# A two-layer decoder on one core: the experts' gate and up weights as stationary operand, head foldings in column halves, one bias product, halved row sums

## What is computed

```python
# layer 0: mixing over time, then attention on a context, then experts
out = jnp.einsum('bes,st->bet', x, Wr + Wc) + bias
...
for e in range(n_experts):                       # 8 experts, one per token
    m = (expert_idx == e)[:, None]
    xe = jnp.where(m, xs, 0.0)
    h = jax.nn.silu(xe @ gate_w[e]) * (xe @ up_w[e])
    out = out + jnp.where(m, h @ down_w[e], 0.0)
# layer 1: Fourier attention, latent attention, ternary feed-forward
q_big = jnp.einsum('bshk,hkq->bshq', q_hk, w_kc_q)
q_r = jnp.einsum('bshq,hqr->bhsr', q_big, W_qr)
k_r = jnp.einsum('bld,hdr->bhlr', kv_rope, W_kr)
scores = jnp.einsum('bhsr,bhlr->bhsl', q_r, k_r)
...
inv = jax.lax.rsqrt(jnp.mean(hf * hf, axis=-1, keepdims=True) + eps)   # rms_norm of h
```

## Time and profile before

| | |
|---|---|
| median of 3 runs | 703.32 us (700.88 to 707.11) |
| profiled execution | 706.16 us |
| its span in the profile | 704.9 us |
| PE busy | 595.1 us, 84% |
| mean granted TensorE clock | 0.935 of 2.4 GHz |

### The profile page before, as it was taken

One profiled execution on the slowest core, in us unless ns is written; L12 is line 12 of the kernel. 1 busy time (PEld: TensorE's weight loads), 2 busy tenths in 40 slices (PEclk: granted clock), 3 DMA queues, 4 the chain that ended last, 5 costly groups with the idle time before them and its releaser, 6 DMA issues.

```text
span 704.9 us, 14612 instructions
## 1 busy us (share of the span) xinstructions
PE 595.1 (84%) x5393; PEld 460.6 (65%) x5393; DVE 503.4 (71%) x1297; ACT 408.1 (58%) x914; POOL 357.3 (51%) x405
## 2 busy tenths in 40 slices
PE   4888788998898775899267789999989999999996
PEld 3655566776666553555233578888768777978885
DVE  3766557776787787556279867777888879968475
ACT  2765456665677752444173356666675766578374
POOL 2435665765549870000398933264484543245565
PEclk9998899999999898999767799999999999999999
DMA  7642212423023422231501000001101010000001
GB/s 235 191 150 75 71 43 85 113 81 99 24 76 124 135 96 90 90 99 61 153 27 45 16 1 2 1 1 32 31 1 31 1 31 3 1 1 2 1 1 61
DMA packets 50416, 41.98 MB, mean 60 GB/s; under 512 B 15513, under 2 KB 48794, under 8 KB 50330
## 3 DMA queue, kind: packets, MB, share of 16 engines
q1 hardware_dynamic: 48810, 36.85, 17.7%
q0 software_dynamic: 1536, 4.20, 1.8%
HBM read 31.72 MB, written 10.35 MB: 60 GB/s over the span
## 4 chain that ended last, share of the span: by engine, by line
PE 42%; DVE 7%; ACT 5%; issue 4%; POOL 2%; DMA 0%; POOLq 0%; DVEq 0%; ACTq 0%
PE bank L1032 8%; PE bank L1034 7%; PE bank L1033 7%; PE bank L1450 6%; PE bank L1039 4%; PE bank L1214 3%; DVE wide L1763 1%; ACT wide L1589 1%; PE bank L1432 1%; PE bank L1315 1%; PE bank L1290 1%; PE bank L1317 1%; PE bank L1288 1%; PE bank L1287 1%; PE bank L1286 1%
## 5 line engine op out<-in xcount | busy, mean ns | idle before, releaser
L1763 DVE TENSOR_TENSOR first<-bank,first 128x512 f16<-128x512 f32 (+3 forms) x113 | 65.3, 592 | 19.4 <-ACT first L1656 6.3
L1039 PE MATMUL bank<-c_identity,wide 128*128 128x128 f32 (+2 forms) x267 | 46.4, 295 | 34.3 <-ACT wide L1589 17.8
L2220 POOL TENSOR_TENSOR first<-first 128x512 f16<-128x512 f32 x44 | 53.0, 1208 | 37.6 <-ACT first L1650 32.4
L1039 PEld LDWEIGHTS bank<-c_identity,wide 128*128 128x128 f32 (+2 forms) x267 | 32.7, 149 | 42.7 <-ACT wide L1589 19.2
L1763 DVE TENSOR_TENSOR wide<-bank,wide 128x512 f16<-128x512 f32 (+3 forms) x85 | 47.0, 566 | 16.1 <-ACT wide L1629 8.5
L1039 PE MATMUL bank<-c_identity,first 128*128 128x128 f32 (+2 forms) x297 | 48.2, 285 | 7.7 <-DVE first L1949 2.4
L2244 POOL DMA_INDIRECT wide<-made_rows,made_at x8 | 8.1, 1007 | 75.3 <-DMA made_rows<-wide 73.5
L1039 PEld LDWEIGHTS bank<-c_identity,first 128*128 128x128 f32 (+2 forms) x297 | 33.7, 140 | 15.3 <-DVE first L1949 3.0
L2200 POOL TENSOR_TENSOR first<-first,minus_half 128x2 f32<-128x2 f32 x30 | 21.5, 717 | 27.8 <-DVE first L1872 27.8
L1032 PE MATMUL bank<-wide,first 128*128 128x256 f16 (+3 forms) x115 | 28.1, 260 | 7.2 <-DVE first L1763 5.9
L2319 POOL TENSOR_TENSOR wide<-wide 128x512 f16<-128x512 f32 x16 | 18.0, 1124 | 31.2 <-ACT wide L1739 31.2
(11 more groups left out here) (509 smaller groups left out, 2249.0 us busy)
## 6 DMA issues: line engine op xcount, KB each, us to landing
wide<-in_L_xattn_Wq SPq DMA_DIRECT2D x9, 256.0 KB, 3.1
wide<-in_L_ffn_gate_w SPq DMA_DIRECT2D x8, 256.0 KB
wide<-in_L_ffn_up_w SPq DMA_DIRECT2D x8, 256.0 KB
wide<-in_L_ffn_down_w SPq DMA_DIRECT2D x8, 256.0 KB
wide<-in_L_xattn_Wo SPq DMA_DIRECT2D x16, 128.0 KB
wide<-in_L_ffn_w_gate_up SPq DMA_DIRECT2D x8, 256.0 KB
first<-in_x SPq DMA_DIRECT2D x7, 256.0 KB, 5.0
x_mid<-first SPq DMA_DIRECT2D x7, 256.0 KB, 3.2
```

Source lines behind the costliest of these rows:

```text
L1039: last = nc.tensor.transpose(view[0:m, c0:c0 + n], src, kc["identity" if dt == F32 else "identity_bf"][0:n, 0:n])
L1763: return V.tensor_tensor(lo, whole, hi, ALU.subtract)
L2220: G.tensor_tensor(B.pl[r], B.pf, B.ph[r], ALU.subtract).then_inc(says("ex_l"), 1)
```

## The change

- Experts: `x_gu` takes the weights as stationary operand, in m = 0 to 3 (two slices of 128 columns of gate, two of up) and c = 0, 1, and the turned tokens as moving one. Its output has h's columns on the partitions, as `x_dn` needs it; `x_b` goes, and `x_b_hi`, `x_b_lo` read h from SBUF.
- Foldings: `hk` turns both heads at once; `hb` puts the two heads on partitions 0 to 63 and 64 to 127 of one bank; `hc` multiplies both by a block-diagonal `krT` (128x128), whose two blocks `hk_c` writes in two copies into zeros set once.
- Bias: it is held on 128 partitions, the high half in row 0, the low in row 1, zeros below, and one matmul adds both.
- `rm`: `ss` of g = 3 also adds the two halves of its 512 columns, and `rm` has half as many matmuls.
- The planner's lengths for these parts are changed, and with them the order of all parts.

```diff
-    p.add("pm_b", 0, 0, "POOL", 110, [("pm_pow", 0, 0)], -10)
+    p.add("pm_b", 0, 0, "POOL", 230, [("pm_pow", 0, 0)], -10)
...
-            p.add("hb", 0, i, "PE", 186, [("ha_c", 0, i)], rank, 1, ("hb_c", 0, i))
+            p.add("hb", 0, i, "PE", 110, [("ha_c", 0, i)], rank, 1, ("hb_c", 0, i))
...
-        chain("x_b", n, 0, [("x_h", n, 0)], k, pe=32, hi=38, lo=42)
+        p.add("x_b_hi", n, 0, "ACT", 38, [("x_h", n, 0)], k)
+        p.add("x_b_lo", n, 0, "DVE", 40, [("x_b_hi", n, 0)], k)
...
-        flip(bank("hk", 0, j), [(n * DC, R, W.kr[:, n, :]) for n in range(HEADS)]).then_inc(says("hk"), 1)
+        flip(bank("hk", 0, j), [(0, P, W.kr.rearrange("p h n -> p (h n)"))]).then_inc(says("hk"), 1)
...
-        for n in range(HEADS):
-            for q in range(2):
-                last = mm(b[0:R, n * D:(n + 1) * D], W.qr[:, q, n, :], k.t1[:, n, q, :], start=(q == 0), stop=(q == 1))
+        for q in range(2):
+            for n in range(HEADS):
+                last = mm(b[n * R:(n + 1) * R, 0:D], W.qr[:, q, n, :], k.t1[:, n, q, :], start=(q == 0), stop=(q == 1))
...
-            for n in range(HEADS):
-                mm(b[:, (2 * c + n) * DC:(2 * c + n + 1) * DC], k.t2[:, n * D + c * P:n * D + (c + 1) * P], k.krT[:, n * DC:(n + 1) * DC],
-                   start=True, stop=True)
+            mm(b[:, c * P:(c + 1) * P], k.t2[:, c * P:(c + 1) * P], k.krT, start=True, stop=True)
...
-                    for half in range(2):
-                        last = mm(o, kc["all_ones"][0:1, :], k.bias[half], start=False, stop=(half == 1))
+                    last = mm(o, kc["all_ones"], k.bias, start=False, stop=True)
...
-        for c in range(C):
-            last = mm3(b[:, :], cut(X.xT, ALL, slice(c * P, (c + 1) * P)), tuple(w[:, c * 2 * D:(c + 1) * 2 * D] for w in gu), c == 0, c == C - 1)
+        for m in range(2 * C):
+            for c in range(C):
+                at = c * 2 * D + m * P
+                last = mm3(b[:, m * P:(m + 1) * P], tuple(w[:, at:at + P] for w in gu), cut(X.xT, ALL, slice(c * P, (c + 1) * P)), c == 0, c == C - 1)
...
-            for n in range(2):
-                last = mm(b[:, t:t + 1], B.ss[:, n * S + t * P:n * S + (t + 1) * P], k.one, start=(n == 0), stop=(n == 1))
+            last = mm(b[:, t:t + 1], B.ss[:, t * P:(t + 1) * P], k.one, start=True, stop=True)
...
     def hk_c(u, j):
         act.wait_ge(*done("hk", 0, j))
-        fn(k.krT, bank("hk", 0, j)[0:R, 0:HEADS * DC], ACT.Copy).then_inc(says("hk_c"), 1)
+        act.wait_ge(*done("pm_pow", 0))
+        for n in range(HEADS):
+            own = slice(n * R, (n + 1) * R)
+            last = fn(k.krT[own, n * DC:(n + 1) * DC], bank("hk", 0, j)[own, 0:DC], ACT.Copy)
...
-        fn(k.t2, bank("hb", 0, j)[0:R, :], ACT.Copy).then_inc(says("hb_c"), 1)
+        fn(k.t2, bank("hb", 0, j)[:, 0:D], ACT.Copy).then_inc(says("hb_c"), 1)
...
+        G.memset(k.krT, 0.0)
...
+        pool.step(G.memset(k.bias, 0.0))
+        pool.step(G.tensor_copy(rows, pre.bias))
+        pool.step(G.tensor_scalar(pre.rest, rows, kc["identity"][0:2, 1:2], None, ALU.mult))
+        G.tensor_tensor(rows, pre.bias, pre.rest, ALU.subtract).then_inc(says("pm_b"), 1)
...
+        last = G.tensor_tensor(B.ss, B.ss, B.s1, ALU.add)
+        if g == 3:
+            pool.step(last)
+            last = G.tensor_tensor(B.ss[:, 0:S], B.ss[:, 0:S], B.ss[:, S:2 * S], ALU.add)
+        last.then_inc(says("ss"), 1)
```

More of the change, by code:

```diff
@@ L141 @@
               "fold_dve": ("hq_lo", "ho_lo"), "ternary_dve": ("f_sc", "f_gt"), "route_dve": ("rt_top", "rt_hot", "rk_seen", "rk_slot"), "gate_act": ("rt_gate", "rt_xs"), "table_dve": ("tb_cnt", "tb_tile", "tb_tok"),
-              "expert_pe": ("x_t", "x_gu", "x_b", "x_dn"), "expert_act": ("x_t_hi", "x_tan", "x_b_hi", "x_out"),
+              "expert_pe": ("x_t", "x_gu", "x_dn"), "expert_act": ("x_t_hi", "x_tan", "x_b_hi", "x_out"),
               "expert_dve": ("x_t_lo", "x_h", "x_b_lo")}
@@ L325, in lay_plan @@
             before = [("ho_lo", 0, i - 1)] if i else []
-            p.add("hk", 0, i, "PE", 25, [("in_h", 0, i), ("in_mix", 0, 0)] + before, rank, 1, ("hk_c", 0, i))
-            p.add("hk_c", 0, i, "ACT", 30, [("hk", 0, i)], rank)
+            p.add("hk", 0, i, "PE", 16, [("in_h", 0, i), ("in_mix", 0, 0)] + before, rank, 1, ("hk_c", 0, i))
+            p.add("hk_c", 0, i, "ACT", 50, [("hk", 0, i), ("pm_pow", 0, 0)], rank)
             p.add("ha", 0, i, "PE", 190, [("in_h", 0, i), ("in_mix", 0, 0)] + before, rank, 2, ("ha_c", 0, i))
@@ L655, in program @@
     k.t1 = wide.tile([HEADS, 2, D], F32, 96)
-    k.t2 = wide.tile([2 * D], F32, R)
+    k.t2 = wide.tile([D])
     k.t3 = wide.tile([2 * D])
-    k.krT = sb("krT", [R, HEADS * DC])[:]
+    k.krT = sb("krT", [P, P])[:]
     wide_end = wide.at
@@ L668, in program @@
     pre.dv = wide.tile([2])
-    pre.bias = wide.tile([S], F32, 1)
+    pre.bias, pre.rest = wide.tile([S], F32, 2), wide.tile([S], F32, 2)
     pre.ones32 = wide.tile([P])
@@ L860, in ld_mix @@
         load(pre.wrow, A["L0_attn_weight"][1:2, :].broadcast_to([P, S]), dma["mix"])
[L861 removed]
+        load(pre.bias, A["L0_attn_bias"].rearrange("(a n) -> a n", a=1).broadcast_to([2, S]), dma["mix"])
         for c in range(C):
@@ L1464, in tensor_program @@
     parts = {f.__name__: f for f in (pm_mm, pt, pd, po, pb, hk, ha, hw, hb, hc, fw, turn, ctx, kv, proj, q, max, mt, sc, pv, ot, rt, rk, sh, tb,
-                                     x_t, x_gu, x_b, x_dn, ft, kt, cs, vt, gu, rm)}
+                                     x_t, x_gu, x_dn, ft, kt, cs, vt, gu, rm)}
     for name, u, g in k.plan.order["PE"]:
@@ L1692, in x_b_hi @@
     def x_b_hi(n, g):
-        act.wait_ge(*done("x_b", n))
-        fn(k.X[n % ELANES].hT[0], bank("x_b", n)[:, 0:D], ACT.Copy).then_inc(says("x_b_hi"), 1)
+        act.wait_ge(*done("x_h", n))
+        fn(k.X[n % ELANES].hT[0], k.X[n % ELANES].h, ACT.Copy).then_inc(says("x_b_hi"), 1)
     def x_out(n, g):
@@ L2095, in x_b_lo @@
         dve.wait_ge(*done("x_b_hi", n))
-        rest(X.hT[1], bank("x_b", n)[:, 0:D], X.hT[0]).then_inc(says("x_b_lo"), 1)
+        rest(X.hT[1], X.h, X.hT[0]).then_inc(says("x_b_lo"), 1)
     def kt_lo(u, g):
```

21 lines of the change are left out of this document (8 added, 13 removed).

## The result

The changed kernel takes 725.33 us (median of 4 runs, 724.08 to 728.65), the kernel before on the same chip 704.53 us. The ratio is 1.031, with a 95% interval of 1.027 to 1.035: slower by 21.6 us, 18.7 to 24.5 on 705. The forecast was 716, slower, with a range of 703 to 729. The profiled execution has a span of 725.1 us where that of before had 704.9.

The account below looks back on a forecast made before the run. PE was taken to lead, with its sequencer's issue bounding the changed experts. Experts +17, clock +1, foldings and bias -4.5, second layer -1 sum to +12.5 us; on 703.3 that gives 716, range 703 to 729.

Parts of the forecast that it names:

- +17 for issue: Expert stage: register instructions make PE's issue the bound, 3.33 us a tile, 84 us for 67.
- +1 for the clock: Expert stage: short falls of PE's granted clock add 1 us.
- issue is hidden: Rival, `x_gu`: a full queue hides issue and the array alone counts, total 694, band 688 to 696; chance 0.08.
- Half clock: Rival, expert stage: clock at 1.2 GHz in part or full, total 725 to 741; chance 0.09.
- Weight loads as the bound: Rival, `x_gu`: weight loads of 0.10 us each set the pace, total 718 at most; chance 0.04.
- The reordered second layer: Rival, second layer: its new order costs its upper bound, total 722; no chance of its own given.
- Foldings and bias: First stretch: PE does 12.7 us less, a third counted, -4.5 us, bounds 0 and -12.7.
- Second layer: Second layer: halved `rm`, longer `ss` and moved order together give -1 us.
- For seven units it lies beside `proj` 3: Second layer: the `ss` fold, 0.65 us on POOL, delays `rm` only in the last unit, +0.5 us with its wait.
- I count -2.5: Second layer: half the `rm` passes go, -3.9 us on PE in all, of which 2.5 counted.
- the order moves here as well, I put +1: Second layer: the moved order of the same parts costs +1 us, between -3 and +7.
- issue-bound experts: Expert stage: the main case, PE's issue sets the pace, total 710 to 725; chance 0.67.

Follow-up runs that it names:

- e6: Changed kernel with expert 0 as a constant for every tile on PE, so no number is loaded or checked and no register instructions remain in the experts: 700.41 us.
- e9: Kernel before with the work of the change's foldings and bias, all planner lengths as before, so the old order: 706.12 us, ratio 1.0004.
- e12: Changed kernel with the old work of foldings and bias, new planner lengths kept, so the changed kernel's order: 734.53 us, ratio 1.045.
- e10: Kernel before, same order, with one more 128x256 fold on POOL at the end of the last `ss`, its result unused: 709.09 us.
- e4: Changed kernel with its halved `rm` and fold in `ss`, but the planner's lengths for both as before: 721.18 us.
- e5: Kernel before with all work as it was, only the planner's lengths of `rm` and the last `ss` set to the new ones: 710.26 us.
- e1: Changed kernel with the experts' part undone, old `x_gu` and `x_b` back: 714.34 us, ratio 1.013.
- e8: Kernel before with foldings and bias of the change, nothing else, in an order of its own: 713.51 us, ratio 1.010.
- e11: Kernel before with foldings and bias of the change and another set of planner lengths, chosen so that the laid out plan is shorter: 714.50 us.
- e2: Kernel before with the experts' part of the change alone: 731.94 us, ratio 1.039.
- e7: Changed kernel with the 23 experts' numbers loaded by three instructions ahead of the first `x_gu`, still 23 checks: 722.34 us, ratio 1.023.

## Why the prediction was right, and where it was not

**The experts: right, by its own steps.** Forecast +17 for issue and +1 for the clock, measured +18.1. A register instruction costs 0.125 us of issue (threes 0.25 apart), the numbers are 368 for 92, and e6 takes the whole away without touching a matmul. A tile takes 3.31 us without waits, for my 3.33, and the waits for DVE and ACT are 3.6 us, for the 4 that I kept. Inside the tile two small errors cancelled: loading and checking takes 0.80 us for my 0.68, and the 0.15 for `x_t` and banks was not needed. The granted clock was 0.98 for 1.00 before: it stood at 0.50 up to 276 us, so the matmuls of the first `x_gu` start 0.107 us apart and it takes 2.5 us for 2.0 by issue. That is half of the +1; from 280 us on the clock was full.

**The rival "issue is hidden": fell** as its own condition said; 0.125 us is not below 0.078. What it would have given is e6: 700.4 measured (694 forecast), the stage 8.8 us shorter than before. The array's share of that is the 4 us of the rival's sum; most of the rest is waits and issue, about 7 us in the stage before and 2.5 in e6. **Half clock: fell** at 0.98 for the stage. **Weight loads as the bound: fell** at 56 ns a matmul in e6. **The reordered second layer, 722:** this one came nearest, with +6.4 us; but the order is only a part of it.

**Foldings and bias: the term of PE right, its share of the end not.** Forecast 12.7 us off PE, measured 13.5; `hb` 1.08 us for 1.15, the four passes of `hc` 0.71 for 0.63. "Of these I count a third" was a guess at how much reaches the end, and there is no such share: in the old order 0 (e9, within 2 us), in the new order some 10, 4 to 16 by the intervals (e12). The sum's -4.5 lies between, and the trace's -2.5 in the stage table is within what one trace can be off.

**Second layer: wrong, -1 forecast, +6.4 measured.** Its stretch was to be shorter by 0 to 5 us. Three steps of it failed, and one was missing. "For seven units it lies beside `proj` 3": the fold took 0.73 us for my 0.65, but PE's waits on `ss` grew from one of 0.6 us to several of 3.6 to 4.5 us, and the layer by 2.1 (e10). I had looked at where the fold stands beside PE's work in the last unit, and not at how little room there was between `ss` and `rm` in the others. "I count -2.5" for the halved `rm`: e4 is not shorter than e10 (350.8 and 350.2), so in the order of before nothing of it is left. The missing step answers for most of it: I took the clock of the last unit for full, and its fall costs e4 1.7 us and e10 nothing, so without it e4 would be about 1 us the shorter one. And "the order moves here as well, I put +1": 2.9 to 3.7 us (e5, after to e4), inside the -3 to +7 that I had given, but that end deserved more weight: of the five new orders in the study (after, e1, e5, e8, e11) none had a shorter second layer.

**Stores and gather, "which the change leaves alone"**: 1.8 us shorter, 15.3 for 17.1. It is 15.2 to 15.8 us in all kernels of the study but before, e2, e5 and e10 (16.6 to 17.3). Those four have the old foldings and bias, but so has e12 with 15.5, and e9 with the old order has 15.3; I can't say why.

The sum of the misses is the difference: 12.5 forecast, and 0.1 more in the experts, 2.0 in the first stretch, 1.8 less behind the experts and 7.4 more in the second layer make 20.2, the difference of the two spans but for rounding.

**The total** was inside the range, 9 us above the 716. It lies at the upper edge of the 710 to 725 that I gave to issue-bound experts, and by the letter in the band of the half clock, 725 to 741, which did not happen. The sum with the second layer at its upper bound gave 722; above that the range rested on the slower clock, so part of the hit is luck: the experts' mechanism and size were right, the second layer's sign was not.

## What to carry to other kernels

Where an operand's address comes from a register, count the distinct slices and not the matmuls: turning the weights into the stationary operand cut them into 16 slices a tile where 4 were enough, and at 0.125 us each the sequencer became slower than the array, which a page of busy times does not show. Read start to start, and compare the issue of a whole tile with its array time before such a change. Where an order is planned from lengths, judge a change in the work and the change in the order apart, by running each alone: here an order alone lengthened the second layer by as much as 6 us, and the order decided whether 13 us less work on the busiest engine were worth some 10 us (4 to 16) or nothing. And where a wait grows, look at the clock behind it: the same 32 matmuls took 5.3 us behind it and 3.65 before.

## What the runs showed of the hardware

- Loading a register from SBUF on PE takes 0.30 us for one number and 0.78 to 1.08 us for seven or eight; a bounds check takes 0.28 us from one to the next (23 in a row in e7), 1.7 times the length of its records.
- Weight loads of 0.10 us each with a matmul of 128 columns behind each can start every 0.056 us (e6): a load's length is not its price.
- Four one-column matmuls behind 1.4 to 2.5 us of idle time were followed by a granted clock of 0.50, and 16 of the next 32 matmuls of 256 columns started 0.213 us apart for 0.109 (e4, after). Eight such matmuls behind 1.44 us of idle time were not (e5).
- On POOL an addition of 128x256 in float32 takes 0.73 us and one of 128x512 1.27: half the size is 57% of the price.
